# Mixture layer behind cross attention: gate rows laid over the partitions by DMA instead of by matmul

## The reference, cut to what matters

```python
def _L0_ffn_ref(x, expert_sel, keys, values):
    sel_logits = jnp.einsum('nd,ed->ne', xt, expert_sel)
    gates = jax.nn.sigmoid(sel_logits)
    sel_val, sel_idx = jax.lax.top_k(gates, N_HEADS)
    gate_full = jnp.zeros_like(gates).at[jnp.arange(N)[:, None], sel_idx].set(sel_val)
    scores = jax.nn.relu(jnp.einsum('nd,edf->nef', xt, keys))
    scores = scores * gate_full[:, :, None]
    out = jnp.einsum('nef,efv->nv', scores, values)
...
x = x + jnp.tanh(g_xattn[0]) * _L0_xattn_ref(ctx_768, _layernorm(x, axis=-1), ...)
x = x + jnp.tanh(g_ffn[0]) * _L0_ffn_ref(_layernorm(x, axis=-1), ...)
```

## Time and profile before

| | |
|---|---|
| median of three executions | 144.35 us |
| the profiled execution, its own time | 143.71 us |
| its span | 141.9 us |
| TensorE busy | 130.3 us, 92% of the span |
| VectorE busy | 105.3 us, 74% |
| ScalarE busy | 72.2 us, 51% |
| GpSimd busy | 9.0 us, 6% |
| mean granted TensorE clock | 0.984 |

### The profile page before, as it was taken

The page is one execution under the profiler, slowest core; times in us unless marked ns, Lnnn a source line. Parts: engine busy times, 40 slices in busy tenths (PEclk is TensorE's granted clock), DMA queues, the critical chain, the costliest instruction groups (busy, mean ns, idle before and its releaser), DMA issues.

```text
span 141.9 us, 2125 instructions
## 1 busy us (share of the span) xinstructions
PE 130.3 (92%) x672; PEld 86.3 (61%) x672; DVE 105.3 (74%) x338; ACT 72.2 (51%) x172; POOL 9.0 (6%) x27
## 2 busy tenths in 40 slices
PE   5999696998889997999899999999999999999990
PEld 5958393585445864878556346366545666676860
DVE  1799969597989785986989643945694689769852
ACT  5368675587682763336234451331214666866620
POOL 7970000000000000000000000000000000000000
PEclk9999999599999999999999999999999999999998
DMA  4697000000000000000000000000000000000004
GB/s 92 206 387 330 9 5 0 2 0 0 0 5 0 0 0 2 5 0 0 0 0 0 5 0 0 0 2 0 0 0 0 0 0 0 7 0 0 0 0 148
DMA packets 2170, 4.27 MB, mean 30 GB/s; under 512 B 240, under 2 KB 1648, under 8 KB 1904
## 3 DMA queue, kind: packets, MB, share of 16 engines
q1 hardware_dynamic: 2160, 4.15, 8.5%
HBM read 3.63 MB, written 0.52 MB: 29 GB/s over the span
## 4 chain that ended last, share of the span: by engine, by line
PE 77%; DMA 7%; DVE 5%; issue 3%; SPq 3%; ACT 2%; DVEq 0%; ACTq 0%
PE bank L907 11%; PE bank L727 11%; PE bank L831 9%; PE bank L729 9%; PE bank L728 8%; PE bank L897 7%; DMA values<-values_in 7%; PE bank L762 3%; PE bank L841 3%; PE bank L785 2%; PE bank L758 2%; PE bank L736 2%; PE bank L772 2%; PE bank L814 2%; PE bank L816 1%
## 5 line engine op out<-in xcount | busy, mean ns | idle before, releaser
L541 DVE SCALAR_TENSOR_TENSOR keys<-bank,inT 128x512 f32<-128x512 f32 x32 | 22.0, 689 | 12.3 <-PE bank L729 11.3
L695 ACT ACTIVATE inT<-bank 128x512 f32<-128x512 f32 x32 | 18.5, 595 | 22.8 <-PE bank L897 22.7
L907 PE MATMUL bank<-keys,values 128*128 128x512 f32 x32 | 16.6, 614 | 0.0
L727 PE MATMUL bank<-xm_hi,k_lo 128*128 128x512 f32 x32 | 15.4, 480 | 0.0
L736 PE MATMUL bank<-ident 128*128 128x128 f32 x96 | 13.6, 297 | 1.5 <-POOL ident L303 1.5
L831 PE MATMUL bank<-prob,proj 128*65 128x256 f32 x64 | 15.0, 382 | 0.0
L736 PEld LDWEIGHTS bank<-ident 128*128 128x128 f32 x96 | 12.9, 212 | 1.8 <-POOL ident L303 1.5
L729 PE MATMUL bank<-xm_hi,k_hi 128*128 128x512 f32 x32 | 12.6, 395 | 0.0
L728 PE MATMUL bank<-xm_lo,k_hi 128*128 128x512 f32 x32 | 12.6, 394 | 0.0
L442 DVE CUSTOM_DVE_ANT_0 junk<-bank,mask_b 128x512 bf16<-128x512 f32 x16 | 10.4, 689 | 3.0 <-PE bank L785 3.0
L897 PE MATMUL bank<-gateT,expand 64*128 64x512 f32 x32 | 11.9, 496 | 0.0
(11 more groups left out here) (133 smaller groups left out, 244.7 us busy)
## 6 DMA issues: line engine op xcount, KB each, us to landing
keys<-keys_in SPq DMA_DIRECT2D x1, 1024.0 KB, 8.1
values<-values_in SPq DMA_DIRECT2D x1, 1024.0 KB, 10.1
out<-x_mid SPq DMA_DIRECT2D x4, 128.0 KB, 1.9
wa<-wa_in SPq DMA_DIRECT2D x1, 320.0 KB, 3.5
vecs_x<-x_in SPq DMA_DIRECT2D x1, 256.0 KB, 5.7
cx<-ctx_in SPq DMA_DIRECT2D x2, 96.0 KB, 2.7
cx<-ctx_in SPq DMA_DIRECT2D x1, 192.0 KB, 5.8
wb<-wb_in SPq DMA_DIRECT2D x1, 145.0 KB, 6.1
```

The costliest lines, as they stand in the source:

```text
L541: dve.scalar_tensor_tensor(hid[:, n % 3, :], bank[H_BANK[n % 2]][:, :], 0.0, gated[:, n % 4, :], ALU.max, ALU.mult).then_inc(hid_ready, 1)
L695: act.activation(gated[:, n % 4, :], gates_bank(n)[:, :], ACT.Copy).then_inc(gated_ready, 1)
L727: pe.matmul(o, ll, rh, start=start, stop=False)
L907: last = pe.matmul(bank[ACC_BANK[h]][:, :], values[:, cc], hid[:, n % 3, :], start=(c == 0), stop=(c == EC - 1))
```

## The change

- `expand`, `one_of`, `spread`, `gates` and VectorE's `turn_gates` are gone. `gate` is written once per token and expert, `gateT` has 32 rows (one per expert) of 1024 tokens in plain fp32, and there are no remainders.
- SP issues 32 DMAs, one per chunk. Each reads rows 2c and 2c + 1 of `gateT`, 512 tokens (2 KB) of each, 64 times over, and writes a slot of `gated`, 128 partitions x 2 KB = 256 KB. The slots are six in place of four, each with a semaphore of its own. The DMA of chunk n waits until VectorE's `up` of chunk n - 6 has freed its slot; the first of each half waits for that half's `gateT`.
- `up` has a third PSUM bank.
- The three order tables are written anew.

```diff
-PAIRS = EC // 2
+SLOTS = 6
...
-        gate = sq[:, 0:2, 0:4, :].rearrange("p i r d -> p i (r d)").rearrange("p i (t q e) -> p i t q e", t=BT, q=4)
-        gateT = sb("gateT", [P, B, S], F32R)
-
-        gated = inT[:, :, :, :].rearrange("p i b s -> p (i b s)").rearrange("p (i n) -> p i n", i=4)
+        gate = sb("gate", [P, NT, E])
+        gateT = sb("gateT", [E, B, S])
+
+        gated = inT[:, :, :, :].rearrange("p i b s -> p (i b s)").rearrange("p (i n) -> p i n", i=SLOTS)
...
-        H_BANK, ACC_BANK = (0, 1), (3, 7)
+        H_BANK, ACC_BANK = (0, 1, 2), (3, 7)
...
+            for h in range(HALF):
+                for b in range(HB * h, HB * h + HB):
+                    sp.wait_ge(gateT_ready, b + 1)
+                for c in range(EC):
+                    n = EC * h + c
+                    if n == 0:
+                        sp.wait_ge(proj_done, 3 * B)
+                    if n >= SLOTS:
+                        sp.wait_ge(hid_ready, n - SLOTS + 1)
+                    sp.dma_start(gated[:, n % SLOTS, :],
+                                 gateT[2 * c:2 * c + 2, HB * h:HB * (h + 1), :].rearrange("e b s -> e (b s)").unsqueeze(1).to_broadcast([2, F, HN])).then_inc(gated_in[n % SLOTS], 16)
...
-                wide = [P, 4, E]
-                for i, j in enumerate(tiles):
-                    last = dve.scalar_tensor_tensor(gate[:, b % 2, i, :, :], left[:, j, 0:E].unsqueeze(1).to_broadcast(wide), TAKEN,
-                                                    sig[:, j, :].unsqueeze(1).to_broadcast(wide), ALU.is_lt, ALU.mult)
-                last.then_inc(gates_ready, 1)
-
-            def turn_gates(b):
-                dve.wait_ge(gateT_ready, b + 1)
-                for row in (E, 3 * E):
-                    rows = slice(row, row + E)
-                    dve.tensor_tensor(gateT[rows, b, :], bank_of(b, TURN_GATES)[rows, 0:S], gateT[rows, b, :].bitcast(F32),
-                                      ALU.subtract).then_inc(gate_lo_ready, 1)
+                dve.scalar_tensor_tensor(gate[:, t, :], left[:, t, 0:E], TAKEN, sig[:, t, :],
+                                         ALU.is_lt, ALU.mult).then_inc(gates_ready, 1)
...
-                dve.wait_ge(gated_ready, n + 1)
+                dve.wait_ge(gated_in[n % SLOTS], 16 * (n // SLOTS + 1))
                 free_hid(n - 3)
-                dve.scalar_tensor_tensor(hid[:, n % 3, :], bank[H_BANK[n % 2]][:, :], 0.0, gated[:, n % 4, :],
+                dve.scalar_tensor_tensor(hid[:, n % 3, :], bank[H_BANK[n % len(H_BANK)]][:, :], 0.0, gated[:, n % SLOTS, :],
                                          ALU.max, ALU.mult).then_inc(hid_ready, 1)
...
-            def gates(h, c):
-                n = EC * h + c
-                if n == 0:
-                    act.wait_ge(proj_done, 3 * B)
-                act.wait_ge(spread_done, n + 1)
-                if n >= 4:
-                    act.wait_ge(hid_ready, n - 3)
-                act.activation(gated[:, n % 4, :], gates_bank(n)[:, :], ACT.Copy).then_inc(gated_ready, 1)
...
-            def spread(h, i):
-                c = i if h == 0 else 2 * i
...
-                for g in range(1 if h == 0 else 2):
-                    rows = slice(2 * E * ((c + g) % 2), 2 * E * ((c + g) % 2) + 2 * E)
-                    pe.matmul(gates_bank(n + g)[:, :], expand[rows, P * (c // 2):P * (c // 2) + P], half(gateT, h)[rows, :],
-                              start=True, stop=True).then_inc(spread_done, 1)
```

More of the change, by code:

```diff
@@ L58 @@
 PE_ORDER = """
[L59 to L73, removed]
@@ L74 @@
-    up 1.12, spread 1.7, up 1.13, down 1.8, down 1.9, up 1.14, up 1.15, down 1.10, down 1.11, down 1.12,
-    down 1.13, down 1.14, down 1.15, finish 0, finish 1
+    warm 0, warm 1, warm 2, warm 3, warm 4, warm 5, warm 6, warm 7, warm 8, warm 9, warm 10, warm 11, turn_in 0,
+    warm 12, project 0, warm 13, turn_in 1, warm 14, warm 15, warm 16, project 1, turn_qk 0, warm 17, warm 18,
+    warm 19, turn_in 2, row_max 0, warm 20, warm 21, project 2, warm 22, warm 23, turn_max 0, turn_qk 1,
+    turn_in 3, weights 0.0, row_max 1, weights 0.1, turn_max 1, project 3, weights 1.0, attend 0.0, turn_qk 2,
@@ new lines @@
+    up 0.11, select 3, up 0.12, down 0.8, down 0.9, turn_gates 2, down 0.10, turn_gates 3, up 0.13, up 0.14,
+    down 0.11, down 0.12, up 0.15, down 0.13, up 1.0, up 1.1, down 0.14, down 0.15, up 1.2, up 1.3, up 1.4,
+    up 1.5, up 1.6, down 1.0, down 1.1, down 1.2, up 1.7, down 1.3, up 1.8, up 1.9, down 1.4, down 1.5, up 1.10,
+    down 1.6, up 1.11, up 1.12, down 1.7, up 1.13, down 1.8, down 1.9, down 1.10, up 1.14, down 1.11, up 1.15,
+    finish 0, down 1.12, down 1.13, down 1.14, down 1.15, finish 1
@@ L83 @@
[L83 to L87, removed]
@@ L94 @@
[L94 to L98, removed]
@@ L99 @@
[L99 to L103, removed]
@@ L104 @@
-    split 1.8, gates 1.12, split 1.9, split 1.10, gates 1.13, finish 0, split 1.11, gates 1.14, split 1.12,
-    gates 1.15, split 1.13, split 1.14, split 1.15, finish 1
+    stats_in 0, turn_in 0, stats_in 1, project 0, stats_in 2, turn_in 1, sum_qk 0, split_values 0, stats_in 3,
+    project 1, turn_qk 0, sum_qk 1, split_values 1, turn_in 2, split_keys 0, project 2, turn_qk 1, weights 0.0,
+    turn_in 3, sum_qk 2, split_keys 1, weights 0.1, project 3, sum_qk 3, split_keys 2, turn_qk 2, turn_qk 3,
@@ L106 @@
+    split 1.10, split 1.11, split 1.12, split 1.13, split 1.14, split 1.15, finish 1
 """
@@ L257, in gated_block @@
         xm_hi_ready, exp_ready, gateT_ready = sem("xm_hi_ready"), sem("exp_ready"), sem("gateT_ready")
-        gated_ready, yT_ready = sem("gated_ready"), sem("yT_ready")
+        yT_ready = sem("yT_ready")
+        gated_in = [sem(f"gated_in{i}") for i in range(SLOTS)]
         inT_done, proj_done, qkT_done = sem("inT_done"), sem("proj_done"), sem("qkT_done")
@@ L263, in gated_block @@
         logit_done, gateT_done = sem("logit_done"), sem("gateT_done")
-        up_done, spread_done, down_done, resT_done = sem("up_done"), sem("spread_done"), sem("down_done"), sem("resT_done")
-        def gates_bank(n):
-            return bank[4 if n >= EC and n % 2 else 2]
+        up_done, down_done, resT_done = sem("up_done"), sem("down_done"), sem("resT_done")
         def turned(b):
@@ L326, in _ @@
             pool.tensor_scalar(mask_b[:, :, 0:S], mask_u8[:, :, :], BIG, -BIG, ALU.mult, ALU.add).then_inc(mask_ready, 1)
[L328 to L333, removed]
         @block.vector
@@ L865, in turn_gates @@
                 for t in range(BT):
-                    src = gate[:, b % 2, t, :, :].rearrange("p q e -> p (q e)")
-                    last = pe.transpose(bank_of(b, TURN_GATES)[:, P * t:P * t + P], src, ident[:, :])
+                    last = pe.transpose(bank_of(b, TURN_GATES)[0:E, P * t:P * t + P], gate[:, BT * b + t, :], ident[:, :])
                 last.then_inc(gateT_done, 1)
@@ L930, in _ @@
                    "turn_mid": turn_mid, "select": select, "turn_gates": turn_gates,
-                   "up": lambda at: up(*at), "spread": lambda at: spread(*at), "down": lambda at: down(*at), "finish": finish}
+                   "up": lambda at: up(*at), "down": lambda at: down(*at), "finish": finish}
             for stage, at in stages(PE_ORDER):
```

73 lines of the change are left out of this document (37 added, 36 removed).

## The result

The changed kernel takes 390.13 us (median of four executions, 387.83 to 391.31) against 144.06 us of the kernel before beside it: a ratio of 2.71, 95% interval 2.69 to 2.73. I had predicted 392 us. Its profiled execution took 387.83 us of its own time, with a span of 385.9 us.

The account below looks back on a forecast made before the run. TensorE was taken to bound the kernel before; after the change, gate DMAs: 70.6 + 1.6 + 32 x 9.67 (309.4) = 381.6 us, plus 8.3 behind and 1.8 around, 392 us predicted, range 236 to 430 us.

Parts of the forecast that it names:

- Where the gates are turned: End of the attention part: the second copy to `gateT` is ready at 70.6 us, 3 us allowed either way.
- The price of a DMA: Gate DMAs of 256 KB: two neighbouring source rows give 27.1 GB/s, so 9.67 us each, bounded below by 0.60 us.
- the case's range: Whole kernel if the source rows limit the gate DMAs: 385 to 429 us, that case's chance 0.48.
- 16 engines or two: Gate DMAs: two source rows outermost, so spreading over 16 engines was doubted; 64 more small packets if two, 512 if all.
- The DMAs follow one another without a gap: Expert stage: compute needs far less than 9.67 us a chunk, so 32 DMAs take 309.4 us, last landing 381.6 us.
- The tail: After the last landing: `up`, two splits, three matmuls at half clock and the 4.9 us end, 8.3 us together.
- TensorE at half clock costs nothing on the path: Expert stage: TensorE falls to 1.2 GHz, doubling its 0.7 us for `up` and for `down`, but stays hidden behind DMAs.
- Rival 2: Gate DMAs on all 16 engines take 0.60 us, hidden; TensorE stays the bound, 133.3 us in all; chance 0.10.
- the 10.4 us of the sum: Expert stage: removed gate-spreading matmuls, 24 x 0.43 us of TensorE's path, upper bound 11.9 us.
- the third bank: PSUM for `up` in the expert stage: lets it run one chunk further ahead, put at nothing.
- Rival 1: Gate DMAs on two engines at full rate, source rows not limiting: 5.42 us each, 255.6 us in all; chance 0.36.
- A sign that didn't show: Gate DMAs' median issue to landing with six queued: near 6 x 9.7 us forecast, 30 us rival 1, 2 us rival 2.

Follow-up runs that it names:

- the faster version: Changed kernel with each DMA reading eight gate rows four partitions apart, so eight engines: 136.4 us, 0.953 of the kernel before; 136.9 us when run again.

## Why the prediction was right, point by point

- **Where the gates are turned**: 70.6 us foreseen, 68.7 us measured, inside the 3 us allowed.
- **The price of a DMA**: 9.67 us taken, the upper end; 9.55 us measured. That the source limits was the choice between two bounds, made at 0.48 against 0.36, and the rows 2, 4, 32 and 64 apart now show it: same engines, same bytes, only the source partitions differ, and the median packet takes 151 or 152 ns in the one case and 84 ns in the other.
- **Luck in that price**: the figure behind it, 27.1 GB/s for 8 partitions, is not what the two rows gave. While both engines read one group a DMA took 10.8 us, 24 GB/s; 9.55 us is the mean with the faster DMAs that the drift brought, which the prediction didn't have. Had the group changed only every fourth chunk, as with rows 32 apart, the time would have been near that kernel's 411 us: inside the case's range of 385 to 429, but 19 us from the forecast. Nor do 8 neighbouring partitions share, if "one sixteenth of the partitions" is taken so: rows 4 apart, within 8 neighbours, didn't. The two rows of the change were close enough for either reading.
- **16 engines or two**: argued from 240 small packets for 15 DMAs and from the outermost counts. Shown: 64 for 32 DMAs with a count of 2, 256 with 8 (496 - 240), and 1024 for the 64 DMAs with one source row and 64 repeats. The Trainium skill, "DMA: Bandwidth & Descriptors", section "Why a DMA increments its semaphore by 16 and not by 1", has this rule of the outermost counts, and all agree.
- **The DMAs follow one another without a gap**: yes. 32 x 9.67 = 309.4 us foreseen, 377.15 - 68.7 = 308.5 us measured from the first issue to the last landing, the first's fixed part in it, for which the sum had 1.6 us more. The tail took 8.8 us for 8.3.
- **TensorE at half clock costs nothing on the path**: the granted clock was 0.55 to 0.59 through the stage, and the first matmul of `up` took 794 ns in the mean, for 480 before; the chain still has the DMAs, with 69% of the span where over 70% was named as a sign.
- **Rival 2's price**: 133.3 us if the transfers were hidden. The version in which they nearly are takes 136.4, the one without most of them 133.2 us. So removing `spread` was sound, and it was the source of the new transfers that undid it. That it is worth the 10.4 us of the sum isn't shown: the 133.2 us also have the third bank, put at nothing but perhaps worth 1 to 5 us, the new orders and the added copies, and no run parts them.
- **Rival 1's price**: 255.6 us; with rows 64 apart it took 252.9, with rows 4 apart 245.8 us. The landings lie 5.1 us apart in both, for 5.42 in the price; the 7 us between the two are those by which the first gate packet started later, at 77.7 and 70.6 us.
- **A sign that didn't show**: the page gives no time from issue to landing for the gate DMAs. It would have been useless, as SP was held in the issue itself (below), so that fewer than the six DMAs of the prediction were out at a time. What replaced it is the gap between two landings.

## What to carry to other kernels

A DMA that lays few rows over many partitions has two prices besides its bytes: how many engines share it, which here followed the outermost counts of its access patterns, and how many groups of SBUF partitions feed it. Count the small packets per DMA in the profile for the first, and for the second give the source as many copies as the pattern can use and put them four partitions apart, not 32. Here four copies of each gate row, eight rows to a DMA and so eight engines, made 390 into 136 us, with two small VectorE copies per 128 tokens; with eight engines but neighbouring rows it was 173 us. A mean can hide two kinds of DMA, here of 10.5 and of 7 us: look at the gaps between landings one by one.

## What was not expected of the hardware

- **SP is held while it issues.** Its instruction for a gate DMA took 9.4 us in the median and 15.4 us at most; in the faster version the median was 0.6 us. The number of 2 KB packets in it isn't the cause: that is the same in both. With one source row and twice as many DMAs of half the size the median was 4.8 us. So SP moves on at about the pace at which the DMA engines finish earlier work. The issue of the fourth DMA ended at 87.2 us, after the first had landed at about 80.8, and whatever stands behind on SP waits too:

```profile
L289 SPq DMA_DIRECT2D inT<-gateT x32: 522/9434/15392, 68.8 to 348.7; - x32
```

- **Partitions 32 apart share like neighbours** when DMAs read them, 152 and 151 ns a packet; with rows 4 and 64 apart it is 84 ns.
- **Two engines on one group drift.** In the change they were never a whole DMA apart, 7.6 us at most of 10.8, and that already took over 1 us off the mean DMA. With the two rows in two groups (64 apart) they stayed together: the DMAs end 5.1 us apart from the first to the last, and both engines with them. Why the lead grows only where they share, no run isolates.
